# Expert 0 split into an early and a late entry around the seam between attention and experts

## The reference, cut to what matters

```python
x = x + tanh(g_xattn) * attention(layernorm(x), ctx, ctx)     # 32 query heads, 8 key/value heads, width 32
x = x + tanh(g_ffn)   * moe(layernorm(x))

# moe, for every row:
scores = softmax(row @ w_cls.T)                 # 64 experts, of which 0..31 are real
topk   = top_k(scores + bias, 8)
w      = scores[topk] / (sum + eps) * 1.5       # entries of experts 32..63 give a factor only
# each real expert takes its rows in row order, at most CAP = 512 of them
gu  = rows @ w_gate_up[e]                       # 1024 -> 2 * 512
act = silu(g) * u
y   = act @ w_down[e]                           # 512 -> 1024
out[row] += w[e] * y * (1 + sum of the w of experts 32..63)
```

## Time and profile before

| what | value |
|---|---|
| median of 3 runs | 2320.85 us (2316.54 to 2320.99) |
| the profiled execution | 2319.56 us, its span 2317.8 us |
| PE busy | 2093.4 us, 90% of the span |
| VectorE, ScalarE, POOL busy | 62%, 52%, 46% |
| granted TensorE clock, mean | 0.973 |

### The profile page before, as it was taken

How to read it: one execution, slowest core, us unless ns; L and a number is a source line. 1 busy time by engine, 2 the same in 40 slices (tenths; PEclk the granted TensorE clock), 3 DMA queues, 4 the chain that set the end, 5 groups by cost and what they waited for, 6 DMA issues and landing times. The chain is left out here.

```text
span 2317.8 us, 47982 instructions
## 1 busy us (share of the span) xinstructions
PE 2093.4 (90%) x14528; PEld 1212.2 (52%) x14529; DVE 1431.3 (62%) x2442; ACT 1216.3 (52%) x1798; POOL 1064.0 (46%) x1228
## 2 busy tenths in 40 slices
PE   5999999999998419899999999999999999999997
PEld 2555554454544214356556574744655776554464
DVE  6788888888886642346545583743464865462374
ACT  3787777676775312235444563633464764353264
POOL 3127888878887560222333262622252644231262
PEclk9999999999999759999999999999999999999998
DMA  5477776767664624556677594975594986766683
GB/s 145 139 181 176 170 186 154 175 169 180 159 149 128 160 78 145 147 130 195 185 192 186 164 291 124 243 217 141 143 280 117 278 238 177 191 170 181 149 216 79
DMA packets 557659, 401.47 MB, mean 173 GB/s; under 512 B 211158, under 2 KB 478550, under 8 KB 557584
## 3 DMA queue, kind: packets, MB, share of 16 engines
q1 hardware_dynamic: 495648, 327.79, 52.2%
q0 software_dynamic: 45184, 72.10, 13.1%
q10 hardware_dynamic: 16752, 0.65, 0.5%
HBM read 310.94 MB, written 101.06 MB: 178 GB/s over the span
## 5 line engine op out<-in xcount | busy, mean ns | idle before, releaser
L1583 PE MATMUL psum<-xgt,wgu 128*128 128x256 f16 (+3 forms) x6144 | 887.4, 302 | 29.1 <-DVE xgt L1334 20.9
L1583 PEld LDWEIGHTS psum<-xgt,wgu 128*128 x6144 | 558.9, 98 | 357.3 <-issue 39.5
L770 POOL TENSOR_TENSOR spare<-spare 128x1 f32<-128x1 f32 x160 | 142.2, 889 | 888.4 <-PE psum L1592 428.7
L1592 PE MATMUL psum<-wdn,apair 128*128 128x512 f16 x1944 | 448.1, 381 | 20.1 <-issue 15.1
L1100 DVE TENSOR_REDUCE mx<-psum 128x2 f32<-128x512 f32 x512 | 328.0, 685 | 89.7 <-PE psum L1438 73.3
L1334 DVE COPY xgt<-psum 128x1024 f16<-128x1024 f16 x256 | 167.4, 684 | 255.3 <-PE psum L1568 232.8
L705 POOL DMA_INDIRECT lists<-entry,dest x256 | 274.0, 1070 | 109.8 <-issue 68.3
L1344 DVE SCALAR_TENSOR_TENSOR a<-psum,sg 128x512 f32<-128x512 f32 x128 | 88.4, 690 | 381.0 <-PE psum L1583 373.4
L894 ACT ACTIVATE prob<-psum 128x512 f32<-128x512 f32 x512 | 277.3, 597 | 68.7 <-PE psum L1451 36.6
L1251 DVE SCALAR_TENSOR_TENSOR wgu<-wraw,wgu 128x1024 f16<-128x1024 f32 x256 | 308.9, 1218 | 4.3 <-ACT wgu L911 4.2
L1592 PEld LDWEIGHTS psum<-wdn,apair 128*128 128x128 f16 x1944 | 184.8, 98 | 220.0 <-issue 27.0
(11 more groups left out here) (154 smaller groups left out, 1918.9 us busy)
## 6 DMA issues: line engine op xcount, KB each, us to landing
wraw<-in_L_ffn_w_gate_up_dram SPq DMA_DIRECT2D x256, 512.0 KB
wraw<-in_L_ffn_w_down_dram SPq DMA_DIRECT2D x128, 512.0 KB
x<-in_x_dram SPq DMA_DIRECT2D x16, 1024.0 KB
xr<-in_x_dram SPq DMA_DIRECT2D x16, 1024.0 KB
out_dram<-x SPq DMA_DIRECT2D x16, 1024.0 KB
pairs<-xs SPq DMA_DIRECT2D x16, 1024.0 KB
qs<-qh SPq DMA_DIRECT2D x248, 64.0 KB
qs<-ql SPq DMA_DIRECT2D x128, 64.0 KB
```

Of the source, the lines that this page charges most:

```text
L1583: mm = pe.matmul(ps_gu[:, s, h, 0:nt * P], w[:, a, k, :], xgt[:, c, k, 0:nt * P], start=(k == 0 and (a, c) == (0, 0)), stop=(k == KB - 1 a ...
L1592: mm = pe.matmul(psum[:, Y_BANK[i] + n2, :], apair[:, o, k, c * P:(c + 1) * P], w[:, a, k, :], start=(k == 0 and (a, o) == (0, 0)), stop=( ...
```

## The change

Expert 0 gets two entries in the list of work, so that there are 33 entries (`nq = ne + 1`). Entry 0, the early one, takes the rows of batches 0 to 11 (`cut = nb - LATE_BATCHES`); entry 1, the late one, takes the rows of batches 12 to 15 with the same weights, loaded again; entry e above that is expert e-1. `positions` of batch 11 sets the base of the slots of expert 0 anew and saves the count. `stage1` is gone.

- **Step 14 and 15.** The slots of `xg` are cleared in step 14. At the start of step 15 SP loads the list of entry 0, POOL gathers its rows in slot 1, PE transposes them and VectorE copies them in slots 3 to 6 (two tiles' halves each). SP loads the gate/up weights early in step 15.
- **Steps 16 and 17.** ScalarE and VectorE split the weights; VectorE's router chain for batch 14 is pulled forward (`router_a` to slot 1, `router_b` to slot 4, `router_w` to slot 7) and carries `gu_lo`, `gate_up` and `act_lo` of entry 0 between its parts. PE's `counts` of batch 14, `logits` and `counts` of batch 15 stand between the products of entry 0 (`up_first`).
- **Entry 1.** Its rows are copied from PSUM to `xgt` by ScalarE (`take_second`) instead of VectorE, between the `y_out` of entry 0.
- **Memory and lists.** `xgt`, `gslots`, `slots` get places that stage one does not use; other tiles are moved.

```diff
+LATE_BATCHES = 4
+    nq = ne + 1
+    cut = nb - LATE_BATCHES
@@ sync, step
+                if at_step(b, nb - 1):
+                    for half_out in lists_out:
+                        sp.wait_ge(half_out, 8 * T2 * TOPK * cut)
+                    get_gslots(0, 0)
+                    sp.dma_start(slots[:, 0], lists_v[0]).then_inc(slots_in[0], 16)
@@ sync, after the steps
             def step2(e, par, last):
                 if is_first(e):
-                    first_wait(sp)
+                    for i in range(CHUNKS):
+                        weights(1, i)
+                    for half_out in lists_out:
+                        sp.wait_ge(half_out, 8 * T2 * TOPK * (nb - 2))
+                    sp.wait_ge(first_out, 2 * 16 * T2)
+                    get_gslots(1, 1)
+                    sp.dma_start(slots[:, 1], lists_v[1]).then_inc(slots_in[1], 16)
+                    for half_out in lists_out:
+                        sp.wait_ge(half_out, 8 * T2 * TOPK * nb)
+                    get_gslots(2, 0)
+                    return
@@ gpsimd
-            gather(0, 0)
-            scatter(nb - 2, nb % 2, 13, T2 * TOPK)
+            scatter(nb - 2, nb % 2, 12, T2 * TOPK)
+            gather(1, 1)
             scatter(nb - 1, 1 - nb % 2, 0, T2 * TOPK)
             for half_out in lists_out:
                 pool.wait_ge(half_out, 8 * T2 * TOPK * nb)
-            gather(1, 1)
             loops2(pool, step2)
@@ scalar
+            def take_second(u):
+
+                c, part = u // 2, u % 2
+                act.wait_ge(gt_full, 8 + u + 1)
+                act.activation(xgt[:, part, :, c * P:(c + 1) * P],
+                               ps_g16[u % 2].rearrange("p (k t) -> p k t", k=KB), ACT.Copy).then_inc(gt_free, 1)
@@ vector, positions
+                if isinstance(b, int) and b == cut - 1:
+                    dve.wait_ge(x_free[x], before("C", step_r(b, "C")) + 1)
+                    tally.add(dve.tensor_scalar(slot0[:, 0:1], carry[:, 0:1], -1.0, float(CAP) - NO_SLOT, ALU.mult, ALU.add))
+                    tally.add(dve.tensor_scalar(before_cut[:], carry[0:1, 0:1], float(CAP), None, ALU.min))
+                    dve.tensor_copy(filled[:, 0:1], carry[0:1, 0:1]).then_inc(filled_set, 1)
@@ vector, step
+                    if 3 <= kv < 7 and at_step(b, nb - 1):
+                        take_t(0, 2 * (kv - 3))
+                        take_t(0, 2 * (kv - 3) + 1)
@@ vector, after the steps
-            dve.memset(spare[:, 4:5], 0.0).then_inc(stage1, 1)
-            dve.wait_ge(stage1, 4)
+            dve.tensor_copy(filled[:, 2:], carry[0:1, 1:]).then_inc(filled_set, 1)
+            dve.tensor_scalar(filled[:, 1:2], carry[0:1, 0:1], float(CAP), before_cut[:], ALU.min, ALU.subtract).then_inc(filled_set, 1)
             def step2(e, par, last):
+                if is_first(e):
+                    dn_lo(0, 0)
+                    dn_lo(0, 1)
@@ tensor
+            def up_first(j, nt):
+
+                pe.wait_ge(gt_free, 2 * nt + FREE)
+                pe.wait_ge(a32_ready, j - 1 + FREE)
+                for h in range(2):
+                    up_half(j, j % 2, wgu[:, j, h].rearrange("p a (k f) -> p a k f", k=KB), nt, h)
+                    if (j, h) == (1, 0):
+                        counts(nb - 2)
+                    if (j, h) == (1, 1):
+                        logits(nb - 1)
+                    if (j, h) == (2, 1):
+                        counts(nb - 1)
```

443 lines of the change are left out of this document (253 added, 190 removed).

## The result

| | before | changed | ratio, 95% interval |
|---|---|---|---|
| median, the chip of the forecast | 2319.95 us (4 runs, 2316.54 to 2320.99) | 2306.44 us (4 runs, 2303.04 to 2308.03) | 0.9939 [0.9927, 0.9951] |
| median, a chip of the other kind (e6_after_again) | 2293.42 us (27 runs) | 2287.75 us (11 runs, 2285.62 to 2291.11) | 0.9978 [0.9969, 0.9987] |

A forecast was written before the change was run, and what follows sets the result against it. PE idles at the seam, so the start of expert 1 counts: PE's chain 909.1 plus 4.9 and 3.8 gives 917.8, 36.7 us earlier; 2319.56 - 36.7 = 2283 us, range 2262 to 2311.

The forecast's parts named there:

- The last attention step ... I take 5: Step 15: added transposes, takes and gather delay the residual by 5 us, to 789.4, within bounds 0 to 16.5.
- H: Follow-up rival for step 15: the transposes and takes themselves cost the time; residual distance 41 us or more, 2286 to 2289.
- Hand-overs ... of which I leave one of 3.8 uncovered: During POOL's train of twenty transfers, hand-overs between other engines come late; one of 3.8 us is added to PE's chain.
- rival (2): Seam: last attention step costs 15, three more hand-overs late by 5; expert 1 25 us later, 2308 us, chance 0.17.
- Then PE enters the loop for the first time, and the 9.72 us ... I charge again: Before the late entry's products: PE's earlier wait at loop entry, without a releaser, recurs at 9.72 us.
- That wait lies before the second half of the first product ... the sum would be the same or up to 5 us more: Entry 0: code fetch at the four-tile branch comes into the open, adding nothing or up to 5 us.
- The late entry: Entry 1: a pass for one empty tile, priced like a one-tile expert at 25.6 us.
- the list chain: Seam: router work, lists, scatters and gathers up to expert 1, putting its first product at 903.3.
- signs of being wrong: Attention ends after 800; expert 0's gate/up passes 850; expert 1's gather lands after 905; expert distances change over 2 us.
- Rival (3): Takes in the last attention step late under POOL's scatters, 57 us instead of 5: 15 us slower, 2335 us, chance 0.08.
- PE's chain: Seam: PE's products of expert 0 and the late pass, up to expert 1 at 909.1, before additions of 4.9 and 3.8.
- Theory F: Follow-up rival on the hold-ups: the holes are PE's loads of its next 16 KB of code, whatever POOL does.

The follow-up runs named there:

- e6_after_again: The changed kernel, unchanged, run on a quiet chip (one without hold-ups): 2287.75 us, ratio 0.9978 to the kernel before.
- e14: Changed kernel with transposes and takes of entry 0's rows moved to slots 5 to 7 of step 15; quiet chip, 2288.06 us, ratio 0.9978.
- e9: Changed kernel with PE running entry 0 straight through its four-tile body, without reading `filled` or branching: 2279.51 us, ratio 0.9937.
- e4: Changed kernel without the late entry (32 entries), expert 1's gather behind all scatters; quiet chip, 2276.36 us, ratio 0.9926.
- e10: Changed kernel without the late entry and without the branch before entry 0: 2265.50 us, ratio 0.9876 to the kernel before.
- e7: Changed kernel with the late entry's rows copied by VectorE instead of ScalarE: 2293.41 us, ratio 1.0002 to the kernel before.

## Why the prediction was right and wrong

Its steps, as distances in us (down products 842.3 - 789.4, and so on), beside the changed kernel on the two kinds of chip:

| step | predicted | hold-ups | quiet |
|---|---|---|---|
| residual of batch 15, later than before | 5 | 15.4 | 7.9 |
| residual to the first down product | 52.9 | 52.2 | 57.6 |
| to the late entry's list on POOL | 10.9 | 6.0 | 6.4 |
| to the list of expert 1 on POOL | 30.6 | 31.0 | 31.4 |
| to the first product of expert 1 | 34.0 | 46.4 | 34.8 |
| start of expert 1 | 917.8 | 935.3 | 917.1 |
| start of expert 1 before | 954.5 | 954.5 | 927.0 |

- **What failed.** On the chip of the forecast expert 1 starts 17.5 us later than forecast: the last attention step costs 10.4 more than its 5, what stands behind the list of expert 1 costs 12.4 more than its 34.0, the late entry's list comes 4.9 sooner, and the two steps left take 0.4 less together. Another 2.7 us are lost behind the start of expert 1, where I cost nothing. Of the two large misses 7.5 and 11.6 us are gone on a quiet chip, so the step that failed is the pricing of hold-ups in the changed kernel: one term of 3.8 us, where the runs show 18.2.
- **Where the time starts from** is the same mistake seen from the other side. I took "954.53" and "a further hole" as the structure of the kernel before, while 27.5 us of it are hold-ups: 5.5 in the last attention step, 20.1 at the takes, the rest within 2 us. I had the rows and used them only for the changed kernel. They are priced into what the change removes and hardly into what it builds. The changed kernel has hold-ups of its own, 18.2 us (935.28 - 917.06), so on such a chip the change trades 27.5 for 18.2.
- **"The last attention step ... I take 5"** was mis-sized: 15.4 where things are held up, 7.9 where not. The bound of 16.5 held. I costed the work and forgot waits: PE's for the gather to land (6.51 us in e6) and VectorE's for `rstd` behind that gather on POOL. But e14 took the first away and won nothing, so the work itself (H) explains the 7.9 at least as well.
- **"Hand-overs ... of which I leave one of 3.8 uncovered"**: rival (2) had the mechanism, ten more us in the last step and three late hand-overs of 5 each behind it. After the residual the trace shows remote waits of 7.03 on `sg` and 14.14 (3.0 of it hold-up), 2.44 and 5.22 on the late rows' copies. From the first late transpose to the late products it took 17.6 us (867.49 to 885.12) instead of 8.5 on the quiet chip. What comes behind the list of expert 1 took 11.6 us longer than there.
- **"Then PE enters the loop for the first time, and the 9.72 us ... I charge again"**: the wait came at another place. Between the opening and the first products of the late pass no wait of PE without a releaser is over 0.36 us in e6, and the loss of 6.58 (7.33 on the first chip) stands at the opening of expert 1. The term was nearly right in size, and its place didn't matter.
- **"That wait lies before the second half of the first product ... the sum would be the same or up to 5 us more"**: the branch to the body of entry 0 costs 8.2 us (e9 against e6). The products had slack, VectorE's list had not.
- **The late entry** at 25.6 us was the price of its work. It costs 11.4 (e4 against e6) to 14.0 us (e10 against e9).
- Right: the late entry is empty; the list chain from the late entry's list to that of expert 1, within 0.8 us on both kinds; "the next thing late after the change is the gather of expert 1" (7.06 us in e6). The clock stays up from 820 to 870 (1.00) and not behind it: 0.66 in 870 to 880 and in 910 to 920, 0.72 in 920 to 930. Two of the signs of being wrong came on the first chip: the gate/up products of expert 0 reach 852.0, and the gather of expert 1 was used at 914. That the sum met 917 on the quiet chip owes much to luck: 2.9 too little for the last step, 4.7 too little to the down products and 1.6 behind the late list, against 4.5 too much for that list and a residual before that stands 5.5 later in the trace I started from.
- Rival (3), takes of 6.4 us in the last attention step, came true in part where there are hold-ups (10.21 us for one take), and not eight times over. Its counter-argument did not hold: POOL issued 13 scatters in a row there. Its rule of two-port copies is not what the takes show: they read PSUM, they wait for PE's transposes, and a scatter beside them takes 0.97 us.
- A slip that changes nothing: the terms to the gather of expert 1 add up to 893.7 and not to 892.7 (the last gather's 0.99 us of the 5.0 lies in the 4.9 as well, so 892.7 is the better number), and PE's chain was the longer one.

What stays open: whether the trains of scatters are the cause of the hold-ups. All nine remote waits of over 5 us in the first chip's two traces, before and after, end in a stretch in which POOL scatters back to back, six times or more, or within 3 us of its end. But the same trains hold up nothing on a quiet chip, and the kernels without them never ran on the other kind. Theory F finds no support in the longest one: from 760 to 771 on the first chip the trace has no packet marked as instruction, and the last one before it took 0.97 us, at 759.12. What the remote waits of VectorE and ScalarE have in common is that the operation behind each reads what PE wrote to PSUM. Also open is what makes expert 1's gather 11 us slower to be used on the first chip (issue at 889.62 to transposes at 914.25, and 883.03 to 896.36 on the quiet one).

## What to carry to other kernels

The hole that a change is meant to fill has to be split before it is counted: what of it is order, and what is a hold-up that the new order will meet again. When work moves under another engine's stage, price the waits that come with it, the landing of its data and the operations that now stand behind it in each in-order queue, and not its busy time alone. A branch is not hidden because its own engine has slack: ask which in-order list elsewhere has the first result of the branch in the middle of it.

## What the hardware showed that I had not expected

- The same kernel differs by 1.1% between chips (2293 and 2317 to 2320 us), and for the kernel before all of it lies ahead of expert 1 (27.5 us there, 26.7 us between the two profiled executions), where VectorE and ScalarE wait beside GpSimd's scatters. The longest that are hold-up in full are 10.21 and 9.79 us.
- ScalarE is held up too, by 9.79 us at 773.62 on the first chip. The Trainium skill (SBUF — State Buffer, Who interferes with whom) says that ScalarE never waits on anyone; it says so of the ports of SBUF. The rows here do not contradict it, since what the operation waits for are PE's products. But the rule does not make an operation of ScalarE prompt.
- The first entry into the branch of entry 0 costs 11.6 us of waiting, and goes with the branch (e9). Waits without a releaser of the same look stand at PE's first opening in the loop (6.6 to 9.8 us) and at the expert behind the loop (5.4 to 7.0); no run took those away.
- A scatter of GpSimd takes 0.97 us beside an idle VectorE or its copies from PSUM, and up to 2.88 beside its splits of weights (e7), ending 0.85 us after the split.
